# Spike-driven feed-forward layer: w2 loaded ahead of x, the idle row summed by VectorE in PSUM, and its adds begun on GpSimd while x arrives

## The reference

```
c      = cond[:, None, :] + cumsum(relu(x) * DT, axis=1)      # DT = 0.001
spikes = (floor(c) - floor(c one token earlier)) / DT
h      = relu(spikes @ w1 + b1)
out    = x + h @ w2 + b2
```

## Time and profile before

| | us |
|---|---|
| median of 3 runs (102.87 to 104.23) | 104.07 |
| span of the profiled execution | 102.1 |
| TensorE busy in it | 95.4 |
| VectorE busy | 65.9 |
| GpSimd busy | 43.2 |
| ScalarE busy | 35.5 |

### The profile page before, as it was taken

The page is one execution under the profiler, slowest core; times in us unless marked ns, Lnnn a source line. Parts: engine busy times, 40 slices in busy tenths (PEclk is TensorE's granted clock), DMA queues, the critical chain, the costliest instruction groups (busy, mean ns, idle before and its releaser), DMA issues.

```text
span 102.1 us, 1157 instructions
## 1 busy us (share of the span) xinstructions
PE 95.4 (93%) x370; PEld 54.0 (53%) x370; DVE 65.9 (64%) x142; ACT 35.5 (35%) x64; POOL 43.2 (42%) x44
## 2 busy tenths in 40 slices
PE   5999999999999999999969999999999999999910
PEld 5944444444644444644234564649999984444300
DVE  2448999888699999488958888899993020020020
ACT  2796515315372540569740000003953330000000
POOL 6350000000078700017508181499937883688040
PEclk9999999999999999999999999999999999999996
DMA  1999999999999999999999725427999999998701
GB/s 58 286 387 414 417 420 411 411 407 409 409 409 409 396 393 401 409 394 387 379 373 352 324 116 218 193 125 292 395 430 436 407 336 195 218 115 106 92 8 62
DMA packets 10028, 31.66 MB, mean 310 GB/s; under 512 B 1671, under 2 KB 1799, under 8 KB 8994
## 3 DMA queue, kind: packets, MB, share of 16 engines
q1 hardware_dynamic: 8304, 29.63, 74.7%
q0 software_dynamic: 1568, 1.90, 11.4%
q10 hardware_dynamic: 146, 0.01, 0.1%
HBM read 21.58 MB, written 10.75 MB: 316 GB/s over the span
## 4 chain that ended last, share of the span: by engine, by line
PE 50%; DVE 20%; POOL 13%; issue 11%; ACT 1%; POOLq 1%; DVEq 0%
PE ps_table L807 40%; DVE x_sb L673 11%; POOL out L347 11%; PE ps_small L900 4%; DVE same L600 3%; PE ps_idle L823 2%; PE ps_turn L844 2%; DVE hot L619 1%; PE ps_idle L827 1%; PE ps_idle L833 1%; DVE spk_t L634 1%; POOL out L381 1%; POOL general_x L370 1%; POOLq L258 1%; DVE spk_t L629 1%
## 5 line engine op out<-in xcount | busy, mean ns | idle before, releaser
L807 PE MATMUL ps_table<-w_sb 128*128 128x512 f32 x128 | 56.9, 595 | 0.0
L807 PEld LDWEIGHTS ps_table<-w_sb 128*128 128x128 f32 x128 | 23.6, 190 | 27.1 <-issue 26.4
L342 POOL DMA_INDIRECT rates<-in_x_turned,sixteen_at x8 | 9.9, 1236 | 33.9 <-DVE sixteen_at L563 32.1
L354 POOL TENSOR_TENSOR x_sb<-x_sb,idle_row 128x512 f32<-128x512 f32 x12 | 14.9, 1277 | 9.9 <-DVEq L706 3.7
L422 ACT ACTIVATE w_sb<-w_sb,b_col 128x512 f32<-128x512 f32 (+2 forms) x19 | 12.2, 643 | 16.5 <-DMA w_sb<-in_w_pairs 16.3
L549 DVE SCALAR_TENSOR_TENSOR total_two<-x_sb,total_two 128x1024 f32<-128x1024 f32 x14 | 17.1, 1225 | 1.2 <-DMA x_sb<-in_x 0.8
L347 POOL DMA_INDIRECT out<-w_sb,to_single x8 | 12.5, 1558 | 5.8 <-issue 3.7
L895 PE MATMUL ps_table<-w_sb 128*128 128x512 f32 x32 | 14.0, 595 | 0.0
L423 ACT ACTIVATE w_sb<-w_sb,minus_relu_b 128x512 f32<-128x512 f32 (+2 forms) x19 | 12.3, 649 | 0.6
L673 DVE TENSOR_TENSOR x_sb<-x_sb,ps_idle 128x2048 f32<-128x2048 f32 x5 | 11.2, 2283 | 1.5 <-ACT idle_row L448 1.3
L895 PEld LDWEIGHTS ps_table<-w_sb 128*128 128x128 f32 x32 | 6.0, 190 | 7.2 <-issue 6.9
(11 more groups left out here) (113 smaller groups left out, 65.5 us busy)
## 6 DMA issues: line engine op xcount, KB each, us to landing
x_sb<-in_x SPq DMA_DIRECT2D x16, 512.0 KB, 14.3
out<-x_sb SPq DMA_DIRECT2D x8, 1024.0 KB, 4.1
w_sb<-in_w_pairs SPq DMA_DIRECT2D x15, 512.0 KB, 15.7
w_sb<-in_w SPq DMA_DIRECT2D x4, 1024.0 KB, 15.3
w_sb<-in_w_pairs SPq DMA_DIRECT2D x2, 256.0 KB, 2.9
b_row<-in_b SPq DMA_DIRECT2D x1, 256.0 KB, 15.3
rates<-in_x_turned,sixteen_at POOLq DMA_INDIRECT x8, 6.5
out<-w_sb,to_single POOLq DMA_INDIRECT x8
```

The lines of the kernel that those rows point to most:

```text
L342: pool.indirect_dma_start(out=rates[:, col, :], out_offset=None, in_=x_sixteen, in_offset=bass.IndirectOffsetOnAxis(ap=sixteen_at[:, col:c ...
L354: last = pool.tensor_tensor(x_sb[b][:, t, :], x_sb[b][:, t, :], idle_row[:, :], ALU.add)
L807: last = pe.matmul(ps_table[c][:, :], table_hidden[:, m, c * P:(c + 1) * P], w2_sb[:, m, :], start=(m == 0), stop=(m == FC - 1))
```

## The change

- **Loads.** w1 turned and w2 are separate tensors, each chunk-major within a partition. w2 comes in eight groups (of 1, 1, 2, 2, 3, 3, 2, 2 chunks), all of them ahead of the first piece of x, with five chunks of w1_turned between. The other eleven chunks of w1_turned follow among x, one for two or three pieces. w1's four parts stand behind the first stores.
- **Idle row.** VectorE makes all 16 chunks, accumulating in PSUM; one TensorE product with a matrix of ones sums over partitions and spreads, and ScalarE copies the row after chunk 4. Strips, join and their tiles go.
- **Totals.** `block_totals` accumulates in a PSUM tile of two banks (the ones of ps_met and ps_small); each step increments `x_summed`.
- **GpSimd's list.** It computes the rise levels and the names (25 small chained steps), then adds the idle row to 24 rows of x: (0, 0 to 9), gathers of batch 0, (0, 10 to 13), gathers of batch 1, (0, 14 and 15), (1, 0 to 7). A row waits only for its x to be summed. `reading_psum` goes. VectorE adds eight rows, (1, 12 to 15) after find_leads(0) and (1, 8 to 11) after the second spikes.
- **Places in TensorE's list** move: sum_idle after chunk 3, sum_totals(0) after chunk 6, sum_totals(1) in the middle of chunk 10, spread_tokens(0) within chunk 11, spread_tokens(1) after two products of chunk 13.

```diff
-            for m in range(3, 8):
-                load_pair(m)
-                load_x(2 * m - 4)
-                if m < 7:
-                    load_x(2 * m - 3)
...
+            load_w1_turned(0)
+            load_w2(0)
+            load_w1_turned(1)
+            load_w2(1)
+            sp.dma_start(start_c[:, :], cond_cols).then_inc(start_in, 16)
+            load_w2(2)
+            load_w1_turned(2)
+            load_w2(3)
+            load_w2(4)
+            load_w1_turned(3)
+            load_w2(5)
+            load_w1_turned(4)
+            load_w2(6)
+            load_w2(7)
+            load_x(0)
+            load_x(1)
+            load_w1_turned(5)
+            for h in range(2, 5):
+                load_x(h)
+            load_w1_turned(6)
+            for h in range(5, 8):
+                load_x(h)
+            load_w1_turned(7)
+            for h in range(8, 11):
+                load_x(h)
+            load_w1_turned(8)
+            for h in range(11, 14):
+                load_x(h)
+            load_w1_turned(9)
+            load_x(14)
+            load_x(15)
+            for m in range(10, FC):
+                load_w1_turned(m)
...
+            store_idle(0, 0)
+            store_idle(0, 1)
+            load_w1(0)
+            load_w1(1)
+            store_idle(0, 2)
+            load_w1(2)
+            load_w1(3)
+            store_idle(0, 3)
+            for q in (0, 3, 1, 2):
+                store_idle(1, q)
...
                 for t in range(begin, end):
+                    pool.wait_ge(x_summed[b], t // TH + 1)
                     last = pool.tensor_tensor(x_sb[b][:, t, :], x_sb[b][:, t, :], idle_row[:, :], ALU.add)
...
             pool.wait_ge(idle_copied, 1)
-            pool.wait_ge(reading_psum, 1)
-            add_idle(0, 12, 14)
-            pool.wait_ge(reading_psum, 2)
+            add_idle(0, 0, 10)
+            get_sixteens(0)
+            add_idle(0, 10, 14)
+            get_sixteens(1)
             add_idle(0, 14, 16)
-            pool.wait_ge(reading_psum, 3)
-            add_idle(1, 12, 16)
-            add_idle(1, 8, 12)
+            add_idle(1, 0, 8)
...
+                if m == 4:
+                    act.wait_ge(idle_summed, 1)
+                    act.activation(idle_row[:, :], ps_idle[:, :], ACT.Copy).then_inc(idle_copied, 1)
+                if m == 7:
                     copy_sums(0)
...
+                step = dve.scalar_tensor_tensor(out=ps_idle[:, :] if m < FC - 1 else idle_part[:, :],
+                                                in0=w2_sb[:, m, :], scalar=relu_b1[:, m:m + 1],
+                                                in1=ps_idle[:, :] if m > 0 else idle_part[:, :], op0=ALU.mult, op1=ALU.add)
...
                     if h == 0:
+                        step = dve.tensor_scalar(sums, tokens, 0.0, None, ALU.max)
                     else:
+                        step = dve.scalar_tensor_tensor(out=sums if h < XH - 1 else total_two[:, :, :], in0=tokens, scalar=0.0,
+                                                        in1=sums, op0=ALU.max, op1=ALU.add)
+                    step.then_inc(x_summed[b], 1)
+                    dve.wait_ge(x_summed[b], h + 1)
...
             first_columns()
+            for m in range(FC):
+                idle_by_hand(m)
+            block_totals(0, 0, XH)
+            block_totals(1, 0, 2)
             find_blocks(0)
+            block_totals(1, 2, 4)
             find_bases(0)
+            block_totals(1, 4, XH)
             find_blocks(1)
             find_tokens(0)
             find_bases(1)
             count_met(0)
             find_leads(0)
-            dve.wait_ge(idle_copied, 1)
-            dve.sem_inc(reading_psum, 1)
-            add_idle(0, 0, 4)
+            add_idle(1, 12, 16)
             find_tokens(1)
             find_slots(0)
             count_met(1)
             find_leads(1)
             first_spikes()
             find_slots(1)
-            dve.sem_inc(reading_psum, 1)
-            add_idle(0, 4, 8)
             second_spikes()
-            add_idle(0, 8, 12)
-            add_idle(1, 0, 4)
-            add_idle(1, 4, 8)
+            add_idle(1, 8, 12)
...
+            def sum_idle():
+                pe.wait_ge(idle_part_ready, 1)
+                pe.matmul(ps_idle[:, :], ones[:, :], idle_part[:, :], start=True, stop=True).then_inc(idle_summed, 1)
...
+            for m in range(2, 4):
+                table_chunk(m)
+            sum_idle()
+            for m in range(4, 7):
+                table_chunk(m)
             sum_totals(0)
+            for m in range(7, 10):
                 table_chunk(m)
+            table_part(10, 0, 2)
             sum_totals(1)
+            table_part(10, 2, DC)
+            table_part(11, 0, 3)
             spread_tokens(0)
+            table_part(11, 3, DC)
+            table_part(12, 0, 3)
             count_leads(0)
             table_part(12, 3, DC)
+            table_part(13, 0, 2)
             spread_tokens(1)
+            table_part(13, 2, DC)
```

214 lines of the change are left out of this document (72 added, 142 removed).

## The result

| | before | after |
|---|---|---|
| median of 4 runs each, us | 104.15 (102.87 to 104.32) | 120.38 (119.92 to 121.49) |
| span of the profiled execution | 102.1 | 118.5 |
| first layer starts at | 68.93 | 84.93 |
| TensorE, VectorE, GpSimd busy | 95.4, 65.9, 43.2 | 98.1, 73.9, 62.1 |

The ratio is 1.162, 95% interval 1.152 to 1.172: slower, as forecast, but by 16.2 us and not by 4.4, and above the range's 115.0. The 16.4 us between the spans lie in the start of the first layer, 16.0; behind it come 33.6 us, 33.2 before.

A forecast was written before the change was run, and what follows sets the result against it. TensorE and the load queue run full in the first half, VectorE's list binds later. The first layer's start moves by +3.6, GpSimd's adds beside VectorE cost 0.9: 104.07 + 3.6 + 0.9 = 108.5 us, range 104.8 to 115.0.

The forecast's parts named there:

- TensorE's saved 3.0: TensorE's list: strips, join and wait removed (3.88 us), one product added (0.86), alone worth -3.0 us.
- The waits of 1.1 and 1.2 on VectorE's list: After the second sum: TensorE waits 1.1 for VectorE's leads, then 1.2 more for batch 1's tokens.
- w1 behind two stores: Load of w1 for the first layer: due by about 67, needed at 72, so moved for nothing.
- the sum's 72.55: Forecast start of the first layer, 47.75 + 9.25 + 4.1 + 11.45, which is +3.6; port term not included.
- the second sum: TensorE's second sum of totals: forecast to end at 47.75, against 43.38 before.
- GpSimd's adds beside VectorE: Ten GpSimd rows stretch four VectorE bursts (leads, tokens, slots, leads) by 0.23 each: 0.9 us, hiding the gathers' 0.5.
- row by row: Rival: each small VectorE step waits for the running GpSimd row, up to 1.2; 7.8 us, total 115.5; chance 0.25.
- the second rival: Rival on load order: loads cost no extras, no port cost, first layer 70 to 71.2, total 104.8 to 106.1; chance 0.18.
- chunk 9's weights: Load order: chunk 9's w1_turned, the 54th unit, reaches ScalarE at 40.2, so TensorE starts chunk 9 at 41.7, before 36.5.
- the wait for the idle row: TensorE after four chunks, at 18.4: waits 1.4 us for VectorE's idle row, ending at 19.9; covered by chunk 9's wait.
- unit 16 of the count: Load count in units of 256 KB, 0.647 us each, from which arrival times of w2, w1_turned and x were forecast.
- the cover: Slack hiding w1's later loading, due by about 67 and needed at 72; without it w1 would cost its lateness.

The follow-up runs named there:

- e1: After, with one wait in GpSimd's list that holds its last ten idle rows until VectorE has built both hot matrices; 109.33 us, ratio 1.056.
- e4: The kernel before without GpSimd's three waits for reading_psum, so its twelve rows run without a pause; 110.67 us, one run.
- t1: After, with GpSimd's last ten rows waiting for VectorE's count_met(0), when it begins find_leads(0); 117.20 us, one run.
- f1: After, with a small GpSimd copy, whose end GpSimd waits for, between batch 1's gathers and the ten rows; 115.28 us, one run.
- e3: After, with two unused VectorE probes: four elements in GpSimd's first run of ten rows, 512 elements ahead of find_leads(0); 121.84 us, one run.
- i1: h1 with all four parts of w1 ahead of the stores in SyncE's list; 110.11 us, ratio 1.066.
- f3: e1 with another load order, one chunk of w1_turned behind every two pieces of x; 109.43 us, ratio 1.058.
- h1: f3 with the four GpSimd rows behind batch 0's gathers also moved behind the wait for both hot matrices; 120.07 us, ratio 1.161.
- h2: h1 with six of VectorE's idle steps and two x steps of each batch left out; 119.73 us, one run.
- e5: The kernel before, old load order, VectorE making all sixteen idle chunks, one product replacing strips and join, two of GpSimd's three waits kept; 106.47 us, ratio 1.028.
- b_fill: The kernel before with one more TensorE product ahead of the strips' join and one more ahead of each later station; 104.24 us, ratio 1.006.
- g3: After, with the same small GpSimd copy as f1 between gathers and rows, but without waiting for it; 120.10 us, one run.

## Why the prediction was wrong

**Right:** the sign, and its reason that TensorE's saved 3.0 would be lost on the way. Reading and writing PSUM costs VectorE nothing (756 ns a step against 750 in the earlier trace rows). ScalarE has chunk 9 at 40.65 (40.2), where the earlier trace rows had 33.78:

```profile
40.65 0.72 ACT L469 ACTIVATE table_hidden<-table_hidden,b_col 128x512 f32<-128x512 f32 x1 [2.58 <-DMA table_hidden<-in_w_turned]
```

The first step of a batch costs 1.22 in PSUM, as taken. The waits of 1.1 and 1.2 on VectorE's list show in e1 (1.10, 1.18). From the second spread to the first layer it is 11.26 (11.45), behind it 33.6 (33.2). w1 behind two stores, put at nothing because it would land by about 67, was worth nothing: in e1 its last part was issued at 50.2 and no part took more than 17.5 to land, so it was there by about 68, and the first layer, at 74.15, didn't wait for it.

The first layer came 12.4 later than the sum's 72.55: 1.3 up to the end of the second sum, 10.4 from there to leads_run, 0.9 from there to the second spread, 0.2 less behind it.

**Wrong, 10.4 us: the step "GpSimd's adds beside VectorE".** It priced "each of four bursts of small steps" at 0.23 and made row by row the upper end. The runs show a third thing: ten rows directly behind gathers are for VectorE one block of 12.2 us. One step paid 10.3, and the later bursts paid nothing because the rows were over. The 0.9 up to the second spread came on top: TensorE was behind VectorE there, its clock still down after the wait. The bound from above came from two stretched instructions of the trace of before, where each portion of rows stands behind a wait; no row there shows rows behind gathers, and I didn't say so. One of the two, the step of 0.42, was read as a case of two SBUF inputs, but it has one (`rates<-rates` in the earlier trace rows). Row by row, which I gave 0.25, holds in e4, t1, f1 and in the first run of ten (e3). It was priced at 7.8, and t1 lost 7.8 and f1 5.7 of first layer against e1. Its own time, 115.5, lay outside the range that was given (up to 115.0, with 0.09 above it): the range didn't fit the chances. A smaller slip: the second rival's first layer at 70 to 71.2 makes 105.1 to 106.3, not 104.8 to 106.1. The Trainium skill, "SBUF — State Buffer", section "Who interferes with whom", has an exclusive lock held for the whole instruction. The steps in t1 (1.26, 1.18) agree with it; those behind gathers (10.47, 5.59, 4.79) do not, and the measurement decides.

**Wrong, 1.3 us, and for another reason: the second sum.** It ended at 49.02, not 47.75. The prediction named chunk 9's weights as the term that decides. They land within half a microsecond of what it said, and alone would let the sum start at 47.3 (40.65, two passes of ScalarE, 12 instructions of TensorE); but three other things stand within a microsecond of that. TensorE's own list reached the sum at 47.7, since the wait for the idle row was 2.26 (1.4 said) and, at the clock granted behind it, the idle row's product and chunks 4 to 6 took 12.95 to the next station where 26 instructions at 0.43 take 11.2. That wait was mis-sized because the idle row ended at 21.1, not 19.9:

```profile
15.62 4.71 DVE L556 SCALAR_TENSOR_TENSOR ps_idle<-w_sb,relu_b,ps_idle 128x512 f32<-128x512 f32 x6 [0.57 <-DMA w_sb<-in_w_rows]
20.37 0.75 DVE L556 SCALAR_TENSOR_TENSOR idle_part<-w_sb,relu_b,ps_idle 128x512 f32<-128x512 f32 x1
```

The group of w2 with chunks 9 to 11, unit 16 of the count and so due at 14.4, let VectorE go on only at 15.6. But the clock alone doesn't decide: in e1 the wait was 1.04, the clock stayed full from 20 to 30, and TensorE reached the sum at 47.6 all the same. VectorE's totals were held by the four rows until 47.96. And VectorE's own steps, which start on x at 21.0 (10.9 before) because sixteen units of w2 come first, ended at 47.0 even with the rows away (i1). The runs show it: the start was 47.8 without the late weights (f3), 47.1 and 47.5 without the rows as well (i1, h1), 47.4 with less of VectorE's work on top (h2). None of these edits, nor three together, brought back the 42.5 of before. What remains of the 5.6 us is then the order that the change makes, w2 ahead of x; that conclusion is argued from the traces, and e5 (old order, 43.05) supports it, but no run moved x alone.

**Right, but only while GpSimd's rows come early:** w1 behind two stores. h1 held the rows that one of these stores waits for, and it cost 9.55 at once. The prediction had said that with the cover gone it would cost what it is late; whoever moves GpSimd's rows must move w1 first.

## What to carry to other kernels

Ask of each run of GpSimd instructions on SBUF what stands directly ahead of it in GpSimd's list, not only how long one takes: here a run behind gathers shut VectorE's steps on two SBUF inputs out until its end, and a small step between them, for whose end GpSimd waited, took 5 us off. Better still is what the kernel before did: release each portion by a mark at the start of a stretch in which VectorE reads PSUM (e4, without these marks, started its first layer 6.5 later). And when several chains end within a microsecond, taking work off one of them is worth nothing: find out with a cheap reordering (b_fill) which list sets the end before paying for the saving on another engine.

## What the runs showed of the hardware

- VectorE's step with two SBUF inputs, of 4 or of 512 elements a partition, lasted 10.47, 11.00, 8.28, 5.59 and 4.79 us under GpSimd adds of 128x512 that followed gathers, and waited for at most one row (1.3) under the same adds behind a kept wait. VectorE's steps with one input in PSUM ran at their usual 0.75 and 1.23 beside both.
- Two inputs are not a condition: in e1, under rows behind a kept wait, tensor_scalar steps with one SBUF input of 8 elements took 1.20 and 1.31, where the kernel before has 0.17 for both.
- Ten rows took 12.22 where they shut VectorE out (g3), and 12.27 where they let it in (t1, f1); there the openings cost GpSimd next to nothing.
- A one-input tensor_scalar of 128x1024 on VectorE took 0.69 into SBUF and 1.22 into PSUM; a scalar_tensor_tensor of 128x512 the same 0.75 into either.
- TensorE's clock in after: behind a wait of 2.26 the stretch from 23 to 26 was granted 0.65 of it; the stretch from 64 to 72, in which a wait of 11.41 ended, 0.50.
